# A group's scaled values moved between its rope turns, the first silu product put behind the first keys' rotation, the packing's low halves on GpSimd, and the first batch's last weights moved by 14 slots

## The reference, cut to what matters

```python
x = x + ln(L0_attn(ln(x)))   # 16 heads of 128, 4 key heads: rope, then linear attention with a decay
x = x + ln(L0_ffn(ln(x)))    # silu(x @ Wg) * (x @ Wu) @ Wd, width 2048, integer weights with scales
x = x + ln(L1_attn(ln(x)))   # 32 heads of 16, 8 key heads: rope on pairs, causal softmax
x = x + ln(L1_ffn(ln(x)))    # x + sigmoid(x @ Wgate) * broadcast, broadcast from the last token
```

## Time and profile before

| what | us |
| --- | --- |
| median of 3 runs | 4074.02 (4072.42 to 4074.05) |
| the profiled execution's own time | 4069.46 |
| its span, first to last instruction | 4067.7 |
| mean granted TensorE clock | 0.957 of full |
| TensorE busy | 3684.8 (91%) |
| VectorE busy | 2525.5 (62%) |
| ScalarE busy | 1505.8 (37%) |
| GpSimd busy | 1359.4 (33%) |

### The profile page before, as it was taken

How to read it: one execution, slowest core, us unless ns; L and a number is a source line. 1 busy time by engine, 2 the same in 40 slices (tenths; PEclk the granted TensorE clock), 3 DMA queues, 4 the chain that set the end, 5 groups by cost and what they waited for, 6 DMA issues and landing times. The chain is left out here.

```text
span 4067.7 us, 51226 instructions
## 1 busy us (share of the span) xinstructions
PE 3684.8 (91%) x18536; PEld 2706.8 (67%) x18536; DVE 2525.5 (62%) x4174; ACT 1505.8 (37%) x2349; POOL 1359.4 (33%) x1674
## 2 busy tenths in 40 slices
PE   6977999999999999999899998999999999977678
PEld 5756776677767776677767776677767776664323
DVE  6654666556674667566664766566664666466347
ACT  4422333434243433434242434434243424315124
POOL 3421452235312551245313541245223541121114
PEclk9988999999999999999999999999999999987789
DMA  6456433254324533254324533353335432332304
GB/s 249 166 215 248 175 129 135 86 205 161 135 84 161 179 122 131 99 205 153 124 94 161 184 106 137 116 204 130 125 105 190 151 134 100 114 106 73 134 14 153
DMA packets 173798, 578.99 MB, mean 142 GB/s; under 512 B 14727, under 2 KB 14983, under 8 KB 168174
## 3 DMA queue, kind: packets, MB, share of 16 engines
q1 hardware_dynamic: 169854, 568.38, 39.3%
q10 hardware_dynamic: 3696, 7.34, 0.5%
HBM read 490.21 MB, written 84.93 MB: 141 GB/s over the span
## 5 line engine op out<-in xcount | busy, mean ns | idle before, releaser
L1892 PE MATMUL ps_P<-XnT_hi,w_ring 128*128 128x512 f32 x3328 | 1084.7, 408 | 60.2 <-DVE silu L1568 24.5
L1892 PEld LDWEIGHTS ps_P<-XnT_hi,w_ring 128*128 128x128 f32 x3328 | 608.5, 192 | 232.1 <-issue 92.3
L1892 PE MATMUL ps_P<-XnT_lo,w_ring 128*128 128x512 f32 x1664 | 659.9, 397 | 0.0
L952 POOL TENSOR_TENSOR hT_lo<-hf,hT_hi 128x512 fp32r<-128x512 f32 x128 | 164.4, 1285 | 935.8 <-ACT hT_hi L1014 935.8
L875 POOL TENSOR_TENSOR pT_lo<-pf,pT_hi 128x512 fp32r<-128x512 f32 x256 | 326.4, 1291 | 358.2 <-ACT pT_hi L1014 358.2
L1160 ACT ACTIVATE probs<-ps_E 128x1024 f32<-128x1024 f32 x320 | 327.5, 1023 | 304.8 <-PE ps_E L2109 304.3
L1558 DVE TENSOR_REDUCE row_max<-ps_T 128x2 fp32r<-128x768 f32 (+3 forms) x448 | 400.1, 917 | 11.0
L1892 PEld LDWEIGHTS ps_P<-XnT_lo,w_ring 128*128 128x128 f32 x1664 | 318.8, 192 | 71.7
L897 POOL TENSOR_SCALAR_AFFINE_SELECT probs<-probs 128x512 f32<-128x512 f32 x256 | 160.0, 637 | 617.2 <-ACT probs L1160 616.1
L1892 PE MATMUL ps_Y<-w_big,hT_hi 128*128 128x512 f32 x896 | 332.0, 417 | 24.8 <-POOL hT_lo L952 11.3
L1551 DVE TENSOR_TENSOR ps_T<-ps_T,mask 128x512 f32<-128x512 f32 (+1 forms) x320 | 187.9, 587 | 230.8 <-PE ps_T L2095 228.9
(11 more groups left out here) (330 smaller groups left out, 7505.0 us busy)
## 6 DMA issues: line engine op xcount, KB each, us to landing
w_ring<-split_dram SPq DMA_DIRECT2D x412, 512.0 KB, 3.5
w_big<-split_dram SPq DMA_DIRECT2D x64, 2048.0 KB, 7.7
dec<-decay SPq DMA_DIRECT2D x32, 1024.0 KB, 5.0
split_dram<-w_ring SPq DMA_DIRECT2D x58, 512.0 KB, 4.4
split_dram<-w_big SPq DMA_DIRECT2D x36, 512.0 KB, 4.3
wo1w<-split_dram SPq DMA_DIRECT2D x8, 2048.0 KB, 7.6
gatew<-split_dram SPq DMA_DIRECT2D x7, 2048.0 KB, 10.8
X<-raw_f SPq DMA_DIRECT2D x46, 256.0 KB, 4.2
```

What stands on the lines that cost most here:

```text
L952: pool.tensor_tensor(hT[1][:, m % IC, :], hf[:, m % 2, :], hT[0][:, m % IC, :].bitcast(F32), ALU.subtract).then_inc(*h_lo.hit(n, m))
L1892: last = pe.matmul(dst, stat[s_], mov[m_], start=first_ and k == 0, stop=last_ and k == n - 1, **kw)
```

## The change

1. `first_pieces`: the o and g pieces move from slots 24 to 31 to slots 38 to 45 of batch 0.
2. `keys_bank`: in batches 0 and 1 the keys of group 0 are turned back in bank E0 instead of Y0.
3. For groups 1 to 3, jobs 0 and 1 go into the rope turns: VectorE scales them behind the rotate of units 2 and 3, ScalarE and GpSimd split them in units 3 and 4. GpSimd's `rstds("pc")` move from units 1 to 4 of group 2 to units 1 and 2 of groups 2 and 3.
4. `layout_low` moves from VectorE to GpSimd, in front of the step's masks, and for group 0 in slot 2 behind the hidden tile's low half.
5. In batches 1 to 7 the first silu product moves from slot 0 to behind the first key tile's rotation.

```diff
@@ first_pieces
-        if 24 <= s < 28:
-            at.append(("o", s - 24))
-        if 28 <= s < 32:
-            at.append(("g", s - 28))
+        if 38 <= s < 42:
+            at.append(("o", s - 38))
+        if 42 <= s < 46:
+            at.append(("g", s - 42))
@@ banks
-        def keys_bank(g):
+        def keys_bank(n, g):
-            return "E0" if g else "Y0"
+            return "E0" if g or n < 2 else "Y0"
@@ gpsimd
+            def job_low(n, g, k):
+                lin = (n * KV0 + g) * NRING + k
+                if lin >= 4:
+                    pool.wait_ge(pv.sem, lin - 3)
+                pool.wait_ge(*p_hi.need(n, g, P_HI[k]))
+                pool.tensor_tensor(pT[1][:, k % 4, :], pf[:, k % 2, :], pT[0][:, k % 4, :].bitcast(F32),
+                                   ALU.subtract).then_inc(*p_lo.hit(n, g, k))
@@ gpsimd rope, behind the sines of unit u
-                    if g == 2 and u and n:
-                        rstds("pc", n - 1, u - 1)
+                    if g and u >= 3:
+                        job_low(n, g, u - 3)
+                    if g >= 2 and u in (1, 2) and n:
+                        rstds("pc", n - 1, 2 * (g - 2) + u - 1)
@@ gpsimd blocks
-                for k in range(NJOB):
...
+                for k in range(2 if g else 0, NJOB):
                     if k < NRING:
...
+                        job_low(n, g, k)
@@ gpsimd, new (on VectorE before)
+            def layout_low(c, g):
+                pool.wait_ge(*q_hi.need(c, g))
+                pool.wait_ge(*rot_sum.need(c, 1, NT - 1))
+                q_ = q_pack[:, :, :, :].rearrange("p t h e -> p (t h) e")
+                pool.tensor_tensor(q_[:, :, 2 * HD1:3 * HD1], R_q[:, g, :, :].rearrange("p t (h d) -> p (t h) d", h=4),
+                                   q_[:, :, 0:HD1].bitcast(F32), ALU.subtract).then_inc(*q_lo.hit(c, g))
+                pool.wait_ge(*k_hi.need(c, g))
+                pool.tensor_tensor(k_pack[:, :, 0::2, HD1:2 * HD1], R_k[:, g, :, :].unsqueeze(2).to_broadcast([P, NT, 2, HD1]),
+                                   k_pack[:, :, 0::2, 0:HD1].bitcast(F32), ALU.subtract).then_inc(*k_lo.hit(c, g))
@@ gpsimd slots
                     if c >= 0:
+                        if s == PREPARE0:
+                            layout_low(c, 0)
                         for i_ in steps_at(s):
+                            if prepare_at(i_) is not None:
+                                layout_low(c, prepare_at(i_))
                             if quad2(i_):
                                 mask_group(c, i_)
@@ scalar rope, behind rope_high of unit u - 1 (job_high: wait for pv and p_f, copy to pT high)
+                    if g and u >= 3:
+                        job_high(n, g, u - 3)
@@ vector rope
                     rotate(n, g, u)
+                    if g and u in (2, 3):
+                        scaled_values(n, g, u - 2)
@@ vector blocks
-                for k in range(2):
-                    if g == 0:
+                if g == 0:
+                    for k in range(2):
                         values_low(n, k)
-                    scaled_values(n, g, k)
-                if g:
+                        scaled_values(n, g, k)
+                else:
                     accumulate(n, g - 1, 0)
                     accumulate(n, g - 1, 1)
@@ vector step and slots: layout_low taken out
@@ vector front
                     for t in range(NT):
                         rotate_pairs(c, 1, t)
+                        if t == 0 and n < NB:
+                            product_out(n, 0)
@@ vector slots
-                    if n < NB and s % 12 < 8:
+                    if n < NB and s % 12 < 8 and (s or c < 0):
                         product_out(n, s)
```

More of the change, by code:

```diff
@@ L864, in rope @@
                         .then_inc(*sine_done.hit(n, g, u))
-                    if g == 2 and u and n:
-                        rstds("pc", n - 1, u - 1)
+                    if g and u >= 3:
+                        job_low(n, g, u - 3)
+                    if g >= 2 and u in (1, 2) and n:
+                        rstds("pc", n - 1, 2 * (g - 2) + u - 1)
             def blocks(n, g):
-                for k in range(NJOB):
[L870 to L873, removed]
+                for k in range(2 if g else 0, NJOB):
                     if k < NRING:
-                        pool.tensor_tensor(pT[1][:, k % 4, :], pf[:, k % 2, :], pT[0][:, k % 4, :].bitcast(F32),
-                                           ALU.subtract).then_inc(*p_lo.hit(n, g, k))
+                        job_low(n, g, k)
                     else:
+                        pool.wait_ge(*p_hi.need(n, g, P_HI[k]))
                         h = slice(2 * (k - NRING), 2 * (k - NRING) + 2)
@@ L1056, in rope_high, with job_high @@
                     .then_inc(*rope_hi.hit(n, g, UNIT_AT[u]))
+            def job_high(n, g, k):
+                lin = (n * KV0 + g) * NRING + k
+                if lin >= 4:
+                    act.wait_ge(pv.sem, lin - 3)
+                act.wait_ge(*p_f.need(n, g, P_F[k]))
+                copy(pT[0][:, k % 4, :], pf[:, k % 2, :]).then_inc(*p_hi.hit(n, g, P_HI[k]))
             def rope(n, g):
@@ L1069, in rope @@
                 act.wait_ge(*proj.need(n, g, KEYS_AT))
-                copy(kv[0][:, :], ps[keys_bank(g)][:, :]).then_inc(*rope_hi.hit(n, g, KEYS_AT))
+                copy(kv[0][:, :], ps[keys_bank(n, g)][:, :]).then_inc(*rope_hi.hit(n, g, KEYS_AT))
                 rope_high(n, g, NU - 1)
@@ L1111, in blocks @@
                                 .then_inc(*o_hi.hit(n, g, h))
-                    lin = (n * KV0 + g) * NRING + k
                     if k < NRING:
[L1114 to L1117, removed]
+                        if k >= 2 or g == 0:
+                            job_high(n, g, k)
                     else:
@@ L1504, in rotate_pairs @@
                 dve.tensor_tensor(dst, dst, b_.rearrange("p (g e) -> p g e", g=KV1), ALU.add).then_inc(*rot_sum.hit(c, part, t))
[L1506 to L1514, removed]
             def step(c, i):
                 at = SLOT_OF[i]
-                if prepare_at(i) is not None:
-                    layout_low(c, prepare_at(i))
                 g = rows_at(i)
@@ L1736, in _ @@
                     if c >= 0:
-                        if s == PREPARE0:
-                            layout_low(c, 0)
                         if steps:
@@ L1929, in keys_back @@
                 pe.wait_ge(*rope_lo.need(n, g, 0))
-                dst = fill(keys_bank(g), rope_hi.need(n, g, KEYS_AT))
+                dst = fill(keys_bank(n, g), rope_hi.need(n, g, KEYS_AT))
                 for t in range(2):
```

## The result

| | median us | runs | ratio to the kernel before |
| --- | --- | --- | --- |
| before | 4074.03 | 4 (4072.42 to 4077.43) | |
| after | 4021.28 | 4 (4019.88 to 4027.52) | 0.9872 [0.9855, 0.989] |

The change is worth -52.7 us; -47 was forecast, 4027 against 4021. The profiled execution of the changed kernel took 4021.19 us with a span of 4019.4: 48.3 less than the span before.

What follows compares the result with a forecast made beforehand. TensorE, busy 91% of the span, was taken as the bound, so only its idle or half-clock time counts. The terms -26 - 17 - 4 + 8 - 8 + 0 = -47 took 4074 to 4027 us; range 4005 to 4055.

Steps and rivals of the forecast that it cites:

- First silu: Front of batches 1 to 7: earlier silu product removes 2.3 us idle and 1.7 half clock; -3.7 a batch, -26 us.
- third rival: TensorE's first gap only moves, slot 3 or packing waiting for GpSimd: 4067 us or within 0.2%; chance 0.1.
- Packing: Second attention: query and key lows leave VectorE, masks start earlier; -2.5 a batch (-17 us), -4 in the last batch.
- Values in the rope turns: Groups 1 to 3, 24 in all: 8.5 us against 8.2 from outputs to output product; +0.35 a group, +8 us.
- The walk: Instruction times through one group's rope turn, VectorE and GpSimd taking turns at SBUF: last query low 2.7 us late.
- first rival: Rope turns: VectorE's next instruction gets in before GpSimd's waiting one; -1.1 a group instead of +0.35, 3992 us; chance 0.2.
- the second (+2.45): Rope turns: one more GpSimd low before a rotate plus a second half-clock period, +2.45 a group, 4086 us; chance 0.1.
- Last weights: Batch 0: moved pieces shorten the third quarter by 16 us and lengthen the fourth by 8; -8 us.
- Keys' bank: Batches 0 and 1: 11.1 us of waits for copied keys go, but the next wait is late; 0 us.

Runs made afterwards that it cites:

- everything on VectorE: The changed kernel with the low halves of jobs 0 and 1 on VectorE instead of GpSimd, products a unit earlier, also VectorE's: 3944.68 us, ratio 0.9691.

## Why the prediction was right, point by point

- **First silu, -3.7 a batch.** Right in mechanism: 247.0 us of slots became 240.8, with packing's 2.5 exactly the sum of the two. The bank was free in time, slot 3 waits 0.23 (0.1 forecast). The third rival (the gap only moves) is out. What was wrong is that the half clock (1.7 of the 3.7) belongs to this gap: with the silu put back the gap is there and no half clock behind it. That this part came true is luck in part. A stretch at half clock about 90 us behind the first tanh stands in one of seven batches of the changed kernel and in six of seven of two other kernels with the silu moved; with six here too, the change would be worth some 8 us less (5 x 1.5).
- **Packing, -2.5 a batch and -4 in the last.** TensorE's waits for the maxima in batch 3's slots went from 5.8 to 3.4, over the whole run from 71.5 to 50.4 (about 50 forecast). In the last stretch the sum was 8.2 instead of 10. On GpSimd the two lows take 0.74 + 0.46 = 1.2 us a group, forecast 1.0:

```profile
L901 POOL TENSOR_TENSOR q_pack<-R_q,q_pack 128x256 fp32r<-128x256 f32 x64 | 47.1, 736 | 308.2 <-ACT q_pack L1034 284.8 <-DVE R_k L1532 21.5
...
L904 POOL TENSOR_TENSOR k_pack<-R_k,k_pack 128x128 fp32r<-128x128 f32 x64 | 29.6, 463 | 0.0
```

- **Values in the rope turns, +0.35 a group.** The walk held nearly instruction by instruction: rotate of the fourth unit 1.77 (1.8 forecast), wait for the last query low 2.58 here and 2.8 in the mean (2.7), waits for `pf` 20.3 (12). Groups 1 and 2 went from 40.85 to 41.15 and 41.2. So the order in a meeting is the one read off, and the first rival (VectorE gets in first) is out, like the second (+2.45). The Trainium skill's page SBUF — State Buffer (Who interferes with whom) calls what VectorE's second SBUF input and GpSimd's reads contend for an exclusive lock. These rows agree: had the two only shared a bandwidth, the rotation's 1.77 would not end 0.54 behind GpSimd's end.
  What the sum missed: over the whole attention part batches 2 to 7 are level with before (206.4 against 206.5 us), since one half-clock stretch behind group 0 went in four of them, which nothing in the forecast foresaw. And in batch 0 the move seems to have cost more than the 1 that I had booked: 221.1 against 215.3 before, and against 211.3 with the values put back. The size is not firm, as four traces with the changed kernel's instructions there range from 217.3 to 223.1, and the 211.3 is of an execution 13.6 us below its median. There VectorE splits weights in the same turns, and TensorE's clock was at half for 6.8 us behind a wait of 3.8.
- **Last weights, -8.** Third quarter 57.6 to 41.4 (42 forecast), fourth 36.8 to 44.0 (45 forecast). Putting the pieces back costs 10.2.
- **Keys' bank, 0.** The waits of 11.1 us became 6.8 for the value piece and 6.5 for the value low, the two named as next; putting the bank back costs 3.5, which is hardly told from 0.
- **The sum and the range.** -47 against -52.7 is closer than its parts: the silu's clock part, the stretch behind group 0 and the two misses of batch 0 all had to fall as they did. The range 4005 to 4055 is also narrower than its own bounds make it: packing's -14 and +26 and the rope turns' -56 and +40 around their terms, added as independent, give 3969 to 4075.

Where the profile could have told more: the forecast weighed whether part 3 pays and took its form as given. The earlier trace rows already shows a low of this shape costing 0.6 on VectorE (issue to issue) and 1.25 on GpSimd, with both inputs in SBUF in either case. Twice the price on a path where both engines queue was visible as the thing to change.

## What to carry to other kernels

Before work goes to GpSimd or is put beside it, add up what both engines do with two SBUF operands in that stretch; the one at 1.27 us delays the other's 0.6 us instruction by up to 1.1, and the page books that as busy. Moving a wait is no gain: 70 us for `pf` turned into 67 us for `qT_lo`, and only the runs that removed the cause gave another 58 to 77 us. Check each removed wait against the next on the same bank, by stage lengths and not by the waits' list.

## What was not expected of the hardware

The half clock does not follow a given gap. Batch 3's slots have the same idle time of 1.73 us at the same place in the changed kernel and in the one with everything on VectorE, and behind it TensorE is busy without a break in both. Once the granted clock stays at 2.4 GHz, once it falls to 1.2 GHz for 3.4 us (timeline, then window, of the changed kernel; below them of the other):

```profile
1606.16 0.50 PE L2125 MATMUL ps_E<-QT,KT 64*128 64x512 f32 x2 [1.73 <-ACT probs L1186]
```

```profile
1606.50:1609.80 3.30, 3.30 (x22) 2.33 (x24) 0.69 (x3) 2.10 (x4) 1.86 (x4) 1.00 0.13 24
```

```profile
1566.99 0.50 PE L2131 MATMUL ps_E<-QT,KT 64*128 64x512 f32 x2 [1.73 <-ACT probs L1183]
```

```profile
1567.50:1570.80 3.30, 3.30 (x10) 2.61 (x11) 0.41 (x2) 1.02 (x1) 1.68 (x3) 0.50 0.00 0
```

What decides between the two is not shown by any run here. Each such stretch makes a stage 1.5 us longer, so the same slots last 240.7 or 242.3 us in one and the same run. An effect of less than 2 us a batch has to be read from idle time and half-clock time apart. In all, TensorE was at half clock for 349 us before, 328 after, and 264 with everything on VectorE.
